# Input projection of a Mamba layer, batch by batch, with the softplus of batch 0 beside it

## The reference

```
proj = hidden_states @ in_proj_w             # 1024 -> 2 * 2048
x, z = split(proj); x, z = (b, 2048, 512) each
xc   = silu(conv_b + sum_k conv_w[k] * x shifted by k)      # 4 taps along l
ssm_p = xc . x_proj_w                        # 2048 -> 64 + 16 + 16
dt_r, Bm, Cm = rmsnorm of the 64, 16, 16 rows
dt   = softplus(dt_proj_w @ dt_r + dt_bias)  # (b, 2048, 512)
h    = exp(dt * A) * h + dt * B * xc         # scan over l
y    = (C . h + D * xc) * silu(z)
```

## Time and profile before

| | |
|---|---|
| time, median of 3 runs | 3049.44 us (3047.0 to 3049.85) |
| span of the profiled execution | 3047.5 us |
| PE, DVE, ACT, POOL busy in the span | 2833.3, 2393.1, 1574.6, 1712.8 us |
| DMA | 445.84 MB, 146 GB/s |

### The profile page before, as it was taken

One profiled execution on the slowest core, in us unless ns is written; L12 is line 12 of the kernel. 1 busy time (PEld: TensorE's weight loads), 2 busy tenths in 40 slices (PEclk: granted clock), 3 DMA queues, 4 the chain that ended last, 5 costly groups with the idle time before them and its releaser, 6 DMA issues. The chain is left out here.

```text
span 3047.5 us, 35696 instructions
## 1 busy us (share of the span) xinstructions
PE 2833.3 (93%) x11958; PEld 2028.4 (67%) x11958; DVE 2393.1 (79%) x2168; ACT 1574.6 (52%) x2685; POOL 1712.8 (56%) x1035
## 2 busy tenths in 40 slices
PE   8997588888788889999999999999989999999997
PEld 7882244444222348888888888887768888887886
DVE  6558999999999977444777777765988888885677
ACT  4448555555665545213888888873433333334443
POOL 0003999999999953403888888861044444430034
PEclk9995799999999999999999999999989999999999
DMA  4228886666875645232111111215245555567654
GB/s 152 83 83 261 274 200 159 179 171 152 250 219 148 199 150 216 104 119 72 37 37 37 37 37 37 71 54 200 97 156 180 180 179 180 180 218 238 194 176 139
DMA packets 217641, 445.84 MB, mean 146 GB/s; under 512 B 33661, under 2 KB 47741, under 8 KB 215613
## 3 DMA queue, kind: packets, MB, share of 16 engines
q1 hardware_dynamic: 179742, 390.73, 41.1%
q10 hardware_dynamic: 37728, 52.96, 5.3%
HBM read 313.45 MB, written 130.15 MB: 146 GB/s over the span
## 5 line engine op out<-in xcount | busy, mean ns | idle before, releaser
L1927 POOL TENSOR_TENSOR at_p_lo<-at_p,at_p_hi 128x512 fp32r<-128x512 f32 x384 | 514.6, 1348 | 244.3 <-ACT at_p_hi L1820 236.5
L716 POOL TENSOR_TENSOR scan_dbx<-scan_u,scan_b_bc 128x1024 f32<-128x1024 f32 x256 | 596.1, 2359 | 0.0
L885 ACT ACTIVATE mamba_ps<-scan_dt,scan_a_neg 128x512 f32<-128x512 f32 (+1 forms) x512 | 332.0, 680 | 315.1 <-DVE scan_g L903 291.3
L914 DVE TENSOR_TENSOR_SCAN mamba_ps<-mamba_ps,scan_dbx 128x1024 f32<-128x1024 f32 x195 | 440.0, 2283 | 3.1 <-ACT mamba_ps L887 1.7
L1847 DVE TENSOR_REDUCE at_neg_max<-heads_ps 128x1 fp32r<-128x1536 f32 x128 | 224.9, 1757 | 134.4 <-PE heads_ps L1939 132.4
L108 PE MATMUL heads_ps<-ff_x_hi,ff_w_hi 128*128 128x512 f32 x784 | 310.0, 395 | 17.2 <-DVE ff_u L2572 6.4
L2812 POOL TENSOR_TENSOR ff_raw<-ff_raw,ff_scale 128x512 f32<-128x512 f32 x112 | 115.9, 1066 | 361.2 <-DMA ff_raw<-in_w 252.8
L109 PE MATMUL heads_ps<-ff_x_lo,ff_w_hi 128*128 128x512 f32 x784 | 308.1, 393 | 0.0
L110 PE MATMUL heads_ps<-ff_x_hi,ff_w_lo 128*128 128x512 f32 x784 | 308.1, 393 | 0.0
L1816 ACT ACTIVATE at_p<-heads_ps 128x512 f32<-128x512 f32 x384 | 228.2, 594 | 110.0 <-PE heads_ps L1963 95.8
L1820 ACT ACTIVATE at_p_hi<-at_p 128x512 fp32r<-128x512 f32 x384 | 242.8, 632 | 12.2
(11 more groups left out here) (306 smaller groups left out, 6906.8 us busy)
## 6 DMA issues: line engine op xcount, KB each, us to landing
scan_dt<-dt SPq DMA_DIRECT2D x120, 256.0 KB, 4.8
scan_u<-u SPq DMA_DIRECT2D x120, 256.0 KB, 7.6
ff_raw<-in_w SPq DMA_DIRECT2D x56, 512.0 KB, 4.6
ff_down_ar<-ac SPq DMA_DIRECT2D x98, 256.0 KB, 2.8
ff_down_hr<-hc SPq DMA_DIRECT2D x98, 256.0 KB, 2.7
ff_act_w<-in_w SPq DMA_DIRECT2D x14, 1024.0 KB, 7.6
hc<-ff_act_t SPq DMA_DIRECT2D x56, 256.0 KB, 6.2
ac<-ff_act_v SPq DMA_DIRECT2D x56, 256.0 KB, 5.9
```

Of the source, the lines that this page charges most:

```text
L716: nc.gpsimd.tensor_tensor(dbx[n % SL][:].rearrange("p (h l) -> p h l", h=2), u[it % 2][:, c:c + 2], b_bc[b][:, k // 2].unsqueeze(1).to_bro ...
L885: nc.scalar.activation(at[:, h * L + h:(h + 1) * L], dt[it % 2][:, c, h:L], ACT.Exp, scale=a_neg[:, it % IT, e:e + 1]).then_inc(a_ready, 1)
L914: nc.vector.tensor_tensor_scan(out[:], ps_a[n % SA], dbx[n % SL][:], 0.0, ALU.mult, ALU.add).then_inc(scanned, 1)
L1927: nc.gpsimd.tensor_tensor(p_lo[n % NSL][:], p[n % NSL][:], f32(p_hi[n % NSL][:]), ALU.subtract).then_inc(p_lo_done, 1)
```

## The change

`mamba_in` is rewritten. Its parts:

- A tile is now one batch: 32 tiles of x (24 matmuls each), first all 16 of batch 0, then those of batch 1, and four tiles of z, all of batch 1. The weights of x are loaded, rounded and split twice. There are three buffers of weights.
- DVE makes the convolution straight from PSUM, 512 elements a step; the copy by ACT is gone. POOL makes the remainders of the weights (1024 elements each). All of `x_proj` is rounded at once.
- A unit of softplus is now two tiles of one batch: units 0 to 7 are batch 0, 8 to 15 batch 1. Units 0 to 7 are made in groups of two, spread over four tiles of batch 1's projection, from tile 18 on. The operand that lay in PSUM (`ps_t`) now lies in SBUF (`dd`). `ee`, `ll`, `dd` and `uu` have two buffers.
- POOL makes the last addition of units 9, 11 and 13.
- SP issues the scan's first loads of dt and u. Before, ACT did.
- The scan makes z of all 16 tiles of batch 0 and 12 of batch 1 (28 as before); the gating of batch 0 starts ten pairs later and comes every 10 pairs instead of 12. Two PSUM pairs of the scan change places.

The diff, cut to its core (helpers named in the text are whole):

```diff
-    NT = 2 * IT - ZN
-    ND = 4
+    NX = B * IT
+    NF = 2 * B
+    NT = NX + NF
+    NG = NX // 2
+    BG = NG // B
+    FIRST_GROUP = IT + 2
+    NW, NX3 = 3, 3
+    ee, ll, dd, uu = ([low(f"{n}{s}", [P, 2, L]) for s in range(2)] for n in ("ee", "ll", "dd", "uu"))
+    main_bank = [ps_all[:, n % 2] for n in range(NX + 2)] + [ps_all[:, 2], ps_all[:, 3]]
+    BY_POOL = (BG + 1, BG + 3, BG + 5)
...
     def sync(sp):
+        def load_w(n):
+            if n >= NW:
+                sp.wait_ge(main_done, n - NW + 1)
+            sp.dma_start(w[n % NW][:], d["w_in"][w_tile(n)]).then_inc(w_ld[n % NW], 16)
+        def store_pair(i):
+            dt_ready(sp, i)
+            sp.dma_start(d["dt"][2 * i:2 * i + 2].rearrange("i p l -> p i l"), dd[i % 2][:]).then_inc(dt_st[i % 2], 16)
+            sp.wait_ge(u_done, i + 1)
+            sp.dma_start(d["u"][2 * i:2 * i + 2].rearrange("i p l -> p i l"), uu[i % 2][:]).then_inc(u_st[i % 2], 16)
+        load_w(0)
+        load_x(0)
+        load_w(1)
...
+        for n in range(NX):
+            if n + NW < NT:
+                load_w(n + NW)
+            store_conv(n)
+            if n == IT:
+                store_bc(0)
+            if n >= FIRST_GROUP + 2 and (n - FIRST_GROUP) % 2 == 1:
+                store_pair(pair)
+                pair += 1
+        load_w(NT - 1)
+        for m in range(2):
+            store_gate(m)
+        sp.wait_ge(xc_st, 16 * NX)
+        scan.load_xs(sp, 0)
+        store_bc(1)
+        sp.wait_ge(xproj_done, NX)
+        scan.load_rows(sp, 0)
+        while pair < BG:
+            store_pair(pair)
+            pair += 1
+        for m in range(2, NF):
+            store_gate(m)
+        sp.wait_ge(main_done, NT)
...
+        scan.load_dt(sp, 0)
+        scan.load_u(sp, 0)
+        scan.load_dt(sp, 1)
+        for i in range(BG, NG):
+            store_pair(i)
+        scan.load_u(sp, 1)
     def scalar(act):
+        round_w(0)
+        for k in range(HT):
+            round_x(0, k)
+        act.wait_ge(par_ld, 16 * 7)
+        round_w(1)
+        nc.scalar.activation(xpw_hi[:], xpw[:], ACT.Copy).then_inc(xpw_hi_done, 1)
+        round_w(2)
+        for n in range(NX):
+            if n:
+                round_w(n + 2)
+            if 0 < n <= HT:
+                round_x(1, n - 1)
+            group, step = divmod(n - FIRST_GROUP, 4)
+            if group >= 0 and step == 0:
+                for i in range(2):
+                    logarithm(2 * group + i)
+            if n == IT:
+                squares(0)
+            silu(n)
+            if n == IT:
+                act.wait_ge(eps_set, 1)
+                root(0)
+            round_xc(n)
+            group, step = divmod(n + 1 - FIRST_GROUP, 4)
+            if group >= 0 and step == 0:
+                for i in range(2):
+                    exponentials(2 * group + i)
...
     def vector(dve):
+        def conv(n):
+            at, m = acc[n % 2], n % IT
+            dve.wait_ge(main_done, n + 1)
+            if n >= 2:
+                dve.wait_ge(xc_done, n - 1)
+            nc.vector.tensor_scalar(at[:], main_bank[n], cw[:, m, KC - 1:KC], cb[:, m:m + 1],
+                                    ALU.mult, ALU.add).then_inc(conv_step, 1)
...
+        def remainder(i):
+            dve.wait_ge(e_done, i + 1)
+            if i >= 2:
+                dve.wait_ge(dt_st[i % 2], 16 * (i // 2))
+                dve.wait_ge(u_done, i - 1)
+            nc.vector.tensor_scalar(dd[i % 2][:], ee[i % 2][:], 1.0, -1.0, ALU.add, ALU.add).then_inc(t_done, 1)
+            dve.wait_ge(t_done, i + 1)
+            nc.vector.tensor_tensor(dd[i % 2][:], ee[i % 2][:], dd[i % 2][:], ALU.subtract).then_inc(c_done, 1)
+        for n in range(NX):
+            conv(n)
+            if n % IT:
+                rest_xc(n - 1)
+            if 0 < n <= HT:
+                rest_x(1, n - 1)
+            if n == IT:
+                normalize(0)
+            group, step = divmod(n - FIRST_GROUP, 4)
+            i = 2 * group
+            if group >= 0 and step == 0:
+                remainder(i)
+            if group >= 0 and step == 1:
+                remainder(i + 1)
+            if n % IT == IT - 1:
+                rest_xc(n)
+            if group >= 0 and step == 1:
+                ramp(i)
+            if group >= 0 and step == 2:
+                ramp(i + 1)
+                total(i)
+            if group >= 0 and step == 3:
+                total(i + 1)
+        ramp(BG - 1)
+        normalize(1)
+        total(BG - 2)
+        total(BG - 1)
+        for i in range(BG, NG, 2):
+            for n in range(2):
+                remainder(i + n)
+            for n in range(2):
+                ramp(i + n)
+                if i + n not in BY_POOL:
+                    total(i + n)
     def gpsimd(pool):
+        def product(i):
+            if i in BY_POOL:
+                pool.wait_ge(c_done, i + 1)
+                pool.wait_ge(r_done, i + 1)
+                nc.gpsimd.tensor_tensor(dd[i % 2][:], dd[i % 2][:], ll[i % 2][:], ALU.add).then_inc(dt_pool, 1)
...
+            nc.gpsimd.tensor_tensor(uu[i % 2][:], dd[i % 2][:], xc[:, 2 * i:2 * i + 2], ALU.mult).then_inc(u_done, 1)
+        for n in range(1, NX + 2):
+            rest_w(n + 2)
+            if n >= FIRST_GROUP + 2 and (n - FIRST_GROUP) % 2 == 0 and pair < BG:
+                product(pair)
+                pair += 1
     def tensor(pe):
+        main(NX)
+        xproj(NX - 2)
+        xproj(NX - 1)
+        main(NX + 1, lambda: mean_squares(1), 2)
+        for i in range(BG, BG + 2):
             dt_product(i)
+        for n in range(NX + 2, NT):
+            main(n)
+        for i in range(BG + 2, NG):
+            dt_product(i)
...
-    GATE_FIRST, GATE_EVERY = 2 * ENDS["z", ZN - 1] + 14, 12
+    GATE_FIRST, GATE_EVERY = 2 * ENDS["z", IT - 1] + 14, 10
-    ps_a = [ps_all[:, m:m + 2].rearrange("p n l -> p (n l)") for m in (6, 0, 4)]
+    ps_a = [ps_all[:, m:m + 2].rearrange("p n l -> p (n l)") for m in (0, 6, 4)]
```

505 lines of the change are left out of this document (239 added, 266 removed).

## The result

The changed kernel takes **3076.82 us** (median of 4 runs, 3075.2 to 3083.95) against 3048.65 (4 runs) for the one before on the same chip: a ratio of 1.0095, interval 1.0081 to 1.0109. It is 28 us slower, where 9 were forecast (3059); the time is inside the range by 0.2 us. The sign was right; the size forecast was a third of what was measured. The profiled execution's span is 3074.2 us against 3047.5.

A forecast was written before the change was run, and what follows sets the result against it. DVE bounds softplus, so the first scan's begin decides: 324.3 plus 3 for the clock is 327.3, 9.1 us later than 318.2, giving span 3056.6, median 3058.5, say 3059. Range 3050 to 3069; 8 in 10 within 3031 to 3077.

The forecast's parts named there:

- What bounds the kernel, and the one number: Whole kernel: PE bounds the projection, DVE softplus; all behind the first scan moves by the same amount as its begin.
- Start: First projection tiles: tile 1 begins at 17.9, 3.5 us late; tile 16 ends at 114.4.
- The price list of a group: Four-tile group: DVE's work 23.5 us, plus store wait 3.0, PE wait 0.7, blocking by POOL about 6.4; 33.5 taken.
- DVE's sum sets the pace: Four-tile groups: DVE's work, waits and blocking add to 33.5 us against PE's 28.0, so DVE sets the pace.
- 0.8 for each of two: PE's clock in the groups: gaps of over 4 us halve it, costing 0.8 us for each of two on the path.
- Rival 3: Groups: the clock stays low, a tile takes 10.3 us, PE becomes the bound; +12, 3071; chance 0.13.
- The tail: Last eight units: with two buffers each pair waits for stores; first scan at 209.9 after tile 16, 324.3 in the span.
- dt(8) lands at 172: Tail: dt(8)'s store, behind three spread loads of 10 us, lands at 172 after tile 16; remainder(10) begins then.
- Rival 2: Tail: stores don't wait behind the loads, dt(8) lands by 166; 6 to 8 us less, 3051; chance 0.10.
- POOL's three additions: Tail: they save DVE 3.7 us, which it spends waiting, and put 2.35 us each into the chain.
- Gating: Scan stage: the same 16 operations, closer together, cost -1 to +3 us, taken as 0.
- Rival 1: Groups and tail: DVE and POOL miss each other, groups take PE's 28 to 28.5 us; 3034; chance 0.30.

The follow-up runs named there:

- a5: The changed kernel with a memset in place of GpSimd's remainders of w from tile 1 on: 3066.58 us, ratio 1.0059.
- a3: The changed kernel with SP issuing the pair stores ahead of the convolution's store: 3064.78 us, ratio 1.0046.
- a9: The changed kernel with both a3's pair stores first and a5's memset for w's remainders: 3064.28 us, ratio 1.0053.
- a2: As a1, with load_rows also moved from ahead of unit 6's store to behind unit 9's: 3070.88 us, ratio 1.0072.
- a1: The changed kernel with the scan's three spread loads issued one at a time behind the stores of units 9, 11 and 13: 3068.91 us, ratio 1.0059.
- a8: As a3, with the scan's loads issued by ScalarE on its own queue instead of SP's: 3057.48 us, ratio 1.0028.
- a6: The changed kernel with VectorE making all eight last additions of batch 1, GpSimd none: 3073.02 us, ratio 1.0078.
- a13: As a11, with all eight last additions on VectorE: 3048.37 us, ratio 1.0000.
- a10: As a8, with four buffers for dt and u from unit 10 on: 3050.89 us, ratio 1.0009.
- a11: As a3, with four buffers for dt and u and all loads in SP's queue, spread among the unit stores: 3051.63 us, ratio 1.0008.
- a14: As a13, with ScalarE rounding tile 1 of w before it waits for the parameters' loads: 3045.40 us, ratio 0.9991.
- a7: The changed kernel with the edits of a1 and a3 together: 3059.61 us, ratio 1.0035.
- a12: The changed kernel with finished y tiles gated every 12 pairs instead of every 10: 3088.99 us, ratio 1.0129.
- a16: As a14, with VectorE instead of GpSimd making w's remainders of tiles 20 to 33: 3051.11 us, ratio 1.0009.

## Why the prediction was right in sign and wrong in size

Two terms of the sum were too small. The half clock in the groups was put at 0.8 us "for each of two", and the store of dt(8) was to land 7 us after its issue, behind the three spread loads; it took 13.0. The groups came out 8.7 us longer and the tail 6.7. One step failed as a mechanism, though its number nearly came out: that DVE's sum of work, stretching and waits sets the pace of a group. That the time lies within 3031 to 3077, by 0.2 us, is luck: the upper end was held open for a rival that didn't come about as told. In detail:

- **What bounds the kernel, and the one number.** Right. Of the 26.7 us that the span grew by, 23.7 are there at the first scan (341.92 against 318.24).
- **Start.** 17.9 for tile 1's begin was 18.6; tile 16's end 2.6 late, total(0) 2.3 late. The gap of 3.5 us was 3.63, and the half clock behind it (some six matmuls 0.43 us apart) is most of the rest; 1.5 was set aside for that.
- **The price list of a group.** Each term came out: stretching 6.7 (6.4), store wait 3.5 (3.0), the tensor_scalar held up. That last one no row showed; the Trainium skill, "SBUF — State Buffer", section "Who interferes with whom", had it held up if it runs in a two-port mode, and the trace agrees with 2.89 us in place of 0.69. **But the step "DVE's sum sets the pace" failed.** It adds the terms, and they don't add: take the stretching by w's remainders away (a5) and the first period stays 34.5; take the store wait away and it is 31.0 (a3); take the stretching and about half of the store wait and it is 31.7 (a9). DVE and PE wait for one another in turn in each tile (conv for the tile, xproj for xc_lo), and a shorter DVE only reaches the next wait sooner: its idle time in the second period grows from 1.9 us (a3) to 10.0 (a9). That the first period came out at 34.5 for 33.5 is partly luck: without the stretching it is 34.5 too, with 1.8 us more wait for the store and 3.1 more for PE (a5).
- **"0.8 for each of two" for the clock in the groups** was the term mis-sized. PE's gaps in the groups were 4.37, 2.37 and 3.58 us. Behind the first two the dt products took 7.03 us instead of 3.60 and the tile after them some 7.5 instead of 5.4. Of that, 1.2 to 2.3 us a period reach the path (a2); with the gaps away (a3), 3.5 us more came back in all than the waits had lasted. Rival 3, which had the clock stay low throughout the groups and cost 12, overstated it: the granted clock was 0.86 and 0.80 there, not 0.5. Of the 8.7 us in this stretch, 1.0 and 3.1 are in the two periods, 1.9 up to xproj(31) (which had PE waiting 3.58), and 2.6 from there to the reciprocal, where ScalarE's root waits 1.47 us for the mean's matmul on a PE whose matmuls are 0.43 us apart.
- **The tail.** The waits named were the right ones: remainder(8) on the rows, remainder(10) on the three spread loads. **"dt(8) lands at 172", 7 us after its issue at about 165, failed: it took 13.0.** I had let the loads' 10 us run from their first issue and the store land behind them, 12.9 us after the last z tile was copied; it took 19.2 (284.5 to 303.7). From remainder(8) to remainder(10) 19.8 us went by, not 15.0. The next two cycles took 9.7 and 12.8 us where 11 and 13.5 were forecast; these two don't follow from the terms beside them (6.4, twice 2.35, 2.8 and about 1 make 14.9). Rival 2, no wait behind the loads, is out: a1 and a8 show the queue's order to matter. At the end, total(15) on DVE (2.34) ran beside the first scan product, and the scan began 3.4 us after the last product of u instead of 2.35. From the reciprocal on that is 1.6 late at remainder(8), 4.8 more at remainder(10), 2.0 won back by remainder(14), and 2.3 lost again up to the scan: 6.7.
- **POOL's three additions** "put 2.35 us each into this chain": each takes 2.35 us ahead of its product of u, and VectorE's saving was worth nothing. But less than that reaches the first scan: with all three on VectorE, at 1.2 us each, the tail is shorter by 2.1 (a6) and 2.9 us (a13) in all.
- **Gating, taken as 0 between -1 and +3.** The profile after has +3.0 behind the first scan, but this column scatters from 2728.7 to 2736.2 us between kernels with the same scan, and a10, a11 and a14 have 2728.7 to 2729.5 with it, the value of before (2729.3). So 0 stands, and 3 of the 17.8 us that the forecast missed are not a cost of the change that these runs could show.
- **Rival 1, DVE and POOL miss each other,** didn't happen. It decided at 2 us of blocking a group, and there were 6.7. But its gain of 5 us a group would hardly have come either: with most of the blocking gone, a9's periods are 31.7 and 33.2, not 28.

The parts, one on top of the other: pair stores first 12.0 us (a3, 3064.8); the loads spread, 17.2 in all (a7, 3059.6); four buffers, 25.2 (a11, 3051.6); no additions on POOL, 28.4 (a13, 3048.4). (a11 spreads the loads otherwise than a7.) That is the whole 28, and the kernel with these four repairs is at the old one's time (3049.2 beside it). With tile 1's weights earlier it is at 3045.4, ratio 0.9991 with an interval up to 1.0000, which isn't a gain that this measurement can tell. The change as such, softplus of batch 0 under the projection, so brought back about what it costs: before, softplus took 87 us from n_done at 231.2 to the first scan; in a14 it takes 57 from about 257.7 on, and the 26 by which n_done is later are read as the dt products and waits that moved into the groups; no run takes them apart.

## What to carry to other kernels

When a stage is put under another one, price its buffers' round trip (work, store, landing, next use) and not its engines: with two buffers the three store waits of 3.5 us in the groups were worth 12 us here (a3) and one of 12 us in the tail was worth 7 (a1), and with two more buffers the two queues tried came out alike. Don't add a stretching and a wait on the same engine without a test: here one was cover for the other, and only taking both away, one by one and together, showed it. And where a wait on one engine leaves TensorE idle for about 2 us, half clock behind it came in some runs and not in others; price the stretch both ways.

## What the runs showed that was not expected

- A store of 0.5 MB issued behind 3 MB of spread loads in the same queue was awaited for 13.0 us; beside the same loads in another engine's queue 9.5; before the change, with a median of 2.7 to 3.8.
- The same gap of TensorE can cost it its clock in one run and not in another. After 2.37 us the granted clock fell to half (1.2 GHz) in the change's second group, with dt products of 7.03 us behind, and held in a1, a2 and a12, with 3.60. Ahead of the first dt products of batch 0, near 127 us, PE waits 2.06 us in most of these kernels: the products then take 3.67 us in the change, a2 and a16, and 5.7 to 6.8 in the others. Total(0) ends at 155.4 to 158.3 in those three and at 158.4 to 161.2 in the others. Between 20 and 265 us PE's gaps of 0.7 to 1.44 us left the clock full in all these runs, and it was at half behind every one of 3.9 us or more.
- A tensor_scalar of one input, SBUF to SBUF, is held up by GpSimd as long as a subtraction of two: 0.69 to 2.89 us.
- Taking the stretching by w's remainders out of every group (a9 against a3) moved nothing (3064.3 against 3064.8 us), while issuing one store ahead of another gave 12 us (a3 against the change).
